# Convolution weights in a ring of six one-bank chunks, first products split by batch, additions spread behind every bank

## The reference

```python
# x: (2, 512, 256), block_values: (128, 64, 64, 16), cols, rows: (128,) in 0..3
xb = x.reshape(batch, n_block_row, 64, t)
x_unfold = xb[:, cols]                      # one block of 64 input channels for each of 128 weights
o = causal_conv1d(x_unfold, block_values)   # 16 taps, 64 in, 64 out, each of the 128 blocks by itself
y = zeros.at[:, rows].add(o)                # summed into the output block that rows names
x = x + y
```

## Time and profile before

| | |
|---|---|
| median of 3 runs | 939.17 us (934.13 to 942.73) |
| profiled execution | 930.08 us, span 928.3 us, mean granted clock 0.996 |
| PE busy | 903.2 us, 97% of the span |
| PEld (weight load) busy | 784.5 us, 85% |
| DVE busy | 540.6 us, 58% |
| ACT busy | 429.8 us, 46% |
| POOL busy | 317.3 us, 34% |
| `wconv` loads | 19 of 1024 KB, 7.3 us to landing; 2 of 512 KB, 4.8 us |
| `wtaps` loads | 16 of 768 KB, 7.9 us to landing |

### The profile page before, as it was taken

The page is one execution under the profiler, slowest core; times in us unless marked ns, Lnnn a source line. Parts: engine busy times, 40 slices in busy tenths (PEclk is TensorE's granted clock), DMA queues, the critical chain, the costliest instruction groups (busy, mean ns, idle before and its releaser), DMA issues. The chain is left out here.

```text
span 928.3 us, 16981 instructions
## 1 busy us (share of the span) xinstructions
PE 903.2 (97%) x5729; PEld 784.5 (85%) x5729; DVE 540.6 (58%) x1360; ACT 429.8 (46%) x945; POOL 317.3 (34%) x286
## 2 busy tenths in 40 slices
PE   9999889999999998999999999999999999999998
PEld 7899757888888886778978997897886888888887
DVE  5899975433333337588678668867875533333333
ACT  3422325433343432576567647646653543433332
POOL 5111012455655563121121202112102256555563
PEclk9999999999999999999999999999999999999999
DMA  8999201111111112000000000000001111111111
GB/s 309 342 354 403 104 11 37 52 51 51 37 48 51 51 34 73 21 23 2 35 23 0 34 0 23 0 0 0 1 1 35 35 52 50 35 51 51 51 34 62
DMA packets 23360, 60.96 MB, mean 66 GB/s; under 512 B 3154, under 2 KB 11028, under 8 KB 20884
## 3 DMA queue, kind: packets, MB, share of 16 engines
q1 hardware_dynamic: 21012, 47.80, 15.4%
q0 software_dynamic: 2304, 12.58, 3.5%
HBM read 59.33 MB, written 1.05 MB: 65 GB/s over the span
## 5 line engine op out<-in xcount | busy, mean ns | idle before, releaser
L822 DVE TENSOR_TENSOR f_h<-f_scaled,bank 128x512 f32<-128x512 f32 (+1 forms) x90 | 60.9, 676 | 183.5 <-POOL f_scaled L723 183.5
L723 POOL TENSOR_TENSOR f_scaled<-f_act,f_gate_rows 128x512 f32<-128x512 f32 (+1 forms) x90 | 113.5, 1262 | 135.5 <-ACT f_act L654 135.1
L912 PE MATMUL bank<-f_xt_hi,f_w_lo 128*128 128x512 f32 (+1 forms) x400 | 157.0, 393 | 0.0
L912 PE MATMUL bank<-f_xt_hi,f_w_hi 128*128 128x512 f32 (+1 forms) x400 | 156.8, 392 | 0.0
L661 ACT ACTIVATE f_h_hi<-f_h 128x512 fp32r<-128x512 f32 (+2 forms) x102 | 63.6, 624 | 183.6 <-DVE f_h L822 183.6
L912 PE MATMUL bank<-f_xt_lo,f_w_hi 128*128 128x512 f32 (+1 forms) x400 | 123.6, 390 | 0.1
L1091 ACT ACTIVATE at_prob<-bank,at_sbias,at_qrs 128x512 f32<-128x512 f32 (+3 forms) x128 | 77.7, 617 | 85.4 <-DVE at_sbias L1261 85.4
L929 PE MATMUL bank<-f_w_lo,f_h_hi 128*128 128x256 f32 (+1 forms) x400 | 113.2, 283 | 0.0
L929 PE MATMUL bank<-f_w_hi,f_h_lo 128*128 128x256 f32 (+1 forms) x400 | 113.1, 283 | 0.0
L929 PE MATMUL bank<-f_w_hi,f_h_hi 128*128 128x256 f32 (+1 forms) x400 | 113.1, 283 | 0.0
L831 DVE TENSOR_TENSOR f_h_lo<-f_h,f_h_hi 128x512 fp32r<-128x512 f32 (+2 forms) x102 | 70.2, 688 | 73.1 <-ACT f_h_hi L661 73.0
(11 more groups left out here) (186 smaller groups left out, 1996.3 us busy)
## 6 DMA issues: line engine op xcount, KB each, us to landing
cv_raw<-in_wconv SPq DMA_DIRECT2D x19, 1024.0 KB, 7.3
cv_shared<-in_wtaps POOLq DMA_DIRECT2D x16, 768.0 KB, 7.9
f_wraw<-in_w SPq DMA_DIRECT2D x44, 256.0 KB, 2.7
f_wraw<-in_w SPq DMA_DIRECT2D x44, 128.0 KB, 2.5
at_wraw<-in_wqkv SPq DMA_DIRECT2D x3, 768.0 KB, 4.3
at_oraw<-in_wo SPq DMA_DIRECT2D x4, 512.0 KB, 3.6
cv_raw<-in_wconv SPq DMA_DIRECT2D x2, 512.0 KB, 4.8
X<-in_x_tiles SPq DMA_DIRECT2D x2, 512.0 KB, 9.0
```

The lines of the kernel that those rows point to most:

```text
L723: g.tensor_tensor(scaled[half][:, cols], act[half][:, cols], gate_rows[:, half * HALF + cols.start:half * HALF + cols.stop], ALU.mult).the ...
L822: v.tensor_tensor(h_f[half][0:rows, cols], src[half][0:rows, cols], pu[half][0:rows, cols], ALU.mult)\
L912: mm = t.matmul(bank[half][0:rows, :], w, x, start=q == 0, stop=q == len(steps) - 1)
```

## The change

The output of the loads, the sums and the products is the same; their sizes and order differ.

- `raw` is a ring of six buffers of one bank each (512 KB) and not three of two banks; SP issues one load per bank, chunk c when chunk c-6 is summed. The host lays `wconv` out in 40 chunks.
- The products of stage 0 are split by batch: those of batch 0 (256 columns) stand between the last four banks of stage 1, those of batch 1 behind them.
- `xn` is two views, one for each batch, each in its own third of `shared`, so that `wtaps` chunk 1 may be loaded after the splits of batch 0 and chunk 2 after those of batch 1.
- The conversion of the block numbers to `line_pair` on DVE moves into stage 0.
- The additions are counted by block: 16 blocks behind stage 1, then 4 behind each low bank of stage 2 and 5 behind each of stages 3 and 4 (`BANK_BLOCKS`). `load_pairs` comes where a block number is a multiple of 8.

```diff
 NPE, ND = 5, 3
-CO, OB, DB = 16, 8, 8
+OB, DB, RING = 8, 8, 6
 
...
         NW = NCB * NCB
-        CHUNK = CO * P
+        CHUNK = OB * P
         DROW = ND * BS
...
         shared = sb("shared", [P, 3 * DB * DROW], F32)
-        xn = shared[:, 0:NT * D].rearrange("p (n t) -> p n t", n=NT)
         raw_d = [shared[:, i * DB * DROW:(i + 1) * DB * DROW].rearrange("p (n f) -> p n f", n=DB) for i in (2, 0, 1)]
+        xn = [shared[:, b * DB * DROW:b * DB * DROW + GC * D].rearrange("p (n t) -> p n t", n=GC) for b in range(B)]
         xc_hi, xc_lo = sb("xc_hi", [P, NCB, B, XPITCH], F32R), sb("xc_lo", [P, NCB, B, XPITCH], F32R)
-        raw = [sb(f"raw{i}", [P, CHUNK], F32) for i in range(3)]
+        raw = [sb(f"raw{i}", [P, CHUNK], F32) for i in range(RING)]
         ws_hi = [sb(f"ws_hi{i}", [P, NW, BS], F32R) for i in range(2)]
...
-        raw_in = [cm(f"cv_raw_in{i}") for i in range(3)]
+        raw_in = [cm(f"cv_raw_in{i}") for i in range(RING)]
-        first_in = [cm(f"cv_first_in{q}") for q in range(CO // OB)]
-        CB = CO // OB
+        FIRST_BLOCKS, BANK_BLOCKS = 2 * DB, (4, 5, 5)
...
             return (lambda x: x[k * BS:(k + 1) * BS, par::2, b, lo:lo + D],
-                    xn[par * BS:(par + 1) * BS, b * GC:(b + 1) * GC, :])
+                    xn[b][par * BS:(par + 1) * BS, :, :])
 
...
         def _(sp):
-            def blocks_first(c):
-                if c >= 3:
-                    sp.wait_ge(s["summed"], (c - 2) * CB)
-                sp.dma_start(raw[c % 3][:], ins["wconv"][c]).then_inc(raw_in[c % 3], 16)
-
-            sp.dma_start(colrow[:, 0:1], ins["cols"].rearrange("(n a) -> n a", a=1)).then_inc(s["cr_in"], 16)
-            sp.dma_start(colrow[:, 1:2], ins["rows"].rearrange("(n a) -> n a", a=1)).then_inc(s["cr_in"], 16)
-            for q in range(CB):
-                part = slice(q * CHUNK // CB, (q + 1) * CHUNK // CB)
-                sp.dma_start(raw[0][:, part], ins["wconv"][0][:, part]).then_inc(first_in[q], 16)
-            blocks_first(1)
-            sp.dma_start(line[:, 0, :], ins["cols"].rearrange("(a n) -> a n", a=1)).then_inc(s["line_in"], 16)
-            sp.dma_start(line[:, 1, :], ins["rows"].rearrange("(a n) -> a n", a=1)).then_inc(s["line_in"], 16)
+            def bank_blocks(c):
+                if c >= RING:
+                    sp.wait_ge(s["summed"], c - RING + 1)
+                sp.dma_start(raw[c % RING][:], ins["wconv"][c]).then_inc(raw_in[c % RING], 16)
+
             def input_half(b):
...
 
+            sp.dma_start(colrow[:, 0:1], ins["cols"].rearrange("(n a) -> n a", a=1)).then_inc(s["cr_in"], 16)
+            sp.dma_start(colrow[:, 1:2], ins["rows"].rearrange("(n a) -> n a", a=1)).then_inc(s["cr_in"], 16)
+            for c in range(3):
+                bank_blocks(c)
+            sp.dma_start(line[:, 0, :], ins["cols"].rearrange("(a n) -> a n", a=1)).then_inc(s["line_in"], 16)
+            sp.dma_start(line[:, 1, :], ins["rows"].rearrange("(a n) -> a n", a=1)).then_inc(s["line_in"], 16)
+            bank_blocks(3)
             input_half(0)
-            blocks_first(2)
+            for c in range(4, 6):
+                bank_blocks(c)
             input_half(1)
-            for c in range(3, NPE * (BS // CO)):
-                blocks_first(c)
+            for c in range(6, NPE * SB):
+                bank_blocks(c)
             prefetch[0](sp)
...
             for d in range(NDC):
-                if d == 1:
-                    g.wait_ge(s["xc_lo_done"], 4 * B)
+                if d in (1, 2):
+                    g.wait_ge(s["xc_lo_done"], 4 * d)
                 if d >= 3:
...
 
-            def add_blocks(d, pairs):
-                v.wait_ge(raw_d_in[d % 3], 16 * (d // 3 + 1))
-                for n in range(DB):
-                    for k in range(2):
-                        v.wait_ge(s["added"], (d * DB + n) * 2 + k + 1)
-                        part = slice(k * DROW // 2, (k + 1) * DROW // 2)
-                        dst = acc[:, bass.ds(pairs[n], 1), part].rearrange("p a f -> p (a f)")
-                        v.tensor_tensor(dst, dst, raw_d[d % 3][:, n, part], ALU.add).then_inc(s["added"], 1)
+            def add_block(i, pairs):
+                d, n = divmod(i, DB)
+                if n == 0:
+                    v.wait_ge(raw_d_in[d % 3], 16 * (d // 3 + 1))
+                for k in range(2):
+                    v.wait_ge(s["added"], i * 2 + k + 1)
+                    part = slice(k * DROW // 2, (k + 1) * DROW // 2)
+                    dst = acc[:, bass.ds(pairs[n], 1), part].rearrange("p a f -> p (a f)")
+                    v.tensor_tensor(dst, dst, raw_d[d % 3][:, n, part], ALU.add).then_inc(s["added"], 1)
 
...
                 for n in range(b * GC, (b + 1) * GC):
-                    v.tensor_scalar(xn[:, n, :], X[:, n, :], moments[:, n, 0:1], rstd[:, n:n + 1],
+                    v.tensor_scalar(xn[b][:, n - b * GC, :], X[:, n, :], moments[:, n, 0:1], rstd[:, n:n + 1],
                                     ALU.subtract, ALU.mult).then_inc(s["xn_ready"], 1)
...
             variances(0)
-            low_banks(0, range(2, 4))
+            v.wait_ge(s["line_in"], 32)
+            v.tensor_copy(line_f[:], line[:]).then_inc(s["cr_conv"], 1)
+            low_banks(0, range(2, 3))
+            v.wait_ge(s["cr_conv"], 3)
+            v.scalar_tensor_tensor(out=line_pair[:], in0=line_f[:, 0, :], scalar=float(NCB), in1=line_f[:, 1, :],
+                                   op0=ALU.mult, op1=ALU.add).then_inc(s["cr_conv"], 1)
+            low_banks(0, range(3, 4))
             normalize(0)
...
             low_banks(1, range(6, 7))
-            v.wait_ge(s["line_in"], 32)
-            v.tensor_copy(line_f[:], line[:]).then_inc(s["cr_conv"], 1)
-            v.wait_ge(s["cr_conv"], 3)
-            v.scalar_tensor_tensor(out=line_pair[:], in0=line_f[:, 0, :], scalar=float(NCB), in1=line_f[:, 1, :],
-                                   op0=ALU.mult, op1=ALU.add).then_inc(s["cr_conv"], 1)
             v.sem_inc(s["added"], 2)
...
             more = load_pairs(1)
-            add_blocks(0, pairs)
-            add_blocks(1, more)
-            d = 2
+            for i in range(DB):
+                add_block(i, pairs)
+            for i in range(DB, FIRST_BLOCKS):
+                add_block(i, more)
+            done = FIRST_BLOCKS
             for st in range(2, NPE):
-                for i in range(4):
-                    low_banks(st, range(2 * i, 2 * i + 1))
-                    pairs = load_pairs(d)
-                    low_banks(st, range(2 * i + 1, 2 * i + 2))
-                    if i == 3 and d + 1 < NDC:
-                        more = load_pairs(d + 1)
-                        add_blocks(d, pairs)
-                        d += 1
-                        pairs = more
-                    add_blocks(d, pairs)
-                    d += 1
+                for q in range(SB):
+                    low_banks(st, range(q, q + 1))
+                    for i in range(done, done + BANK_BLOCKS[st - 2]):
+                        if i % DB == 0:
+                            pairs = load_pairs(i // DB)
+                        add_block(i, pairs)
+                    done += BANK_BLOCKS[st - 2]
             for st in range(NPE, NST):
...
             def sum_bank(st, q):
-                c, part = st * (BS // CO) + q // CB, q % CB
-                if c > 0 and part == 0:
-                    t.wait_ge(raw_in[c % 3], 16 * (c // 3 + (c % 3 > 0)))
-                if st * SB + q >= BANKS:
-                    t.wait_ge(s["ws_lo_done"], st * SB + q - BANKS + 1)
-                if c == 0:
-                    t.wait_ge(first_in[part], 16)
+                c = st * SB + q
+                t.wait_ge(raw_in[c % RING], 16 * (c // RING + 1))
+                if c >= BANKS:
+                    t.wait_ge(s["ws_lo_done"], c - BANKS + 1)
                 for o in range(OB):
-                    w0 = (part * OB + o) * P
                     m = t.matmul(ps[q % BANKS][:].rearrange("p (w o) -> p w o", o=OB)[:, :, o],
-                                 raw[c % 3][:, w0:w0 + P], onehot[:], start=True, stop=True)
+                                 raw[c % RING][:, o * P:(o + 1) * P], onehot[:], start=True, stop=True)
                 m.then_inc(s["summed"], 1)
 
-            def products(slot, c, r, tap):
+            def products(slot, c, r, tap, half=None):
                 w = c * NCB + 2 * r
-                hi, lo = (x[:, c, :, bass.ds(tap, D)] for x in (xc_hi, xc_lo))
+                batch = slice(0, B) if half is None else slice(half, half + 1)
+                bank = ps[4 + r][:, batch.start * D:batch.stop * D]
+                hi, lo = (x[:, c, batch, bass.ds(tap, D)] for x in (xc_hi, xc_lo))
                 w_hi, w_lo = (x[slot][:, w:w + 2, :].rearrange("p c o -> p (c o)") for x in (ws_hi, ws_lo))
                 for lhs, rhs in ((w_hi, hi), (w_lo, hi), (w_hi, lo)):
-                    t.matmul(ps[4 + r][:], lhs, rhs, start=False, stop=False)
```

(23 more changed lines are left out.)

## The result

| | before | after |
|---|---|---|
| median of the runs | 937.0 us (933.74 to 946.46, 20 runs) | 932.07 us (931.08 to 933.35, 20 runs) |
| ratio after to before | | 0.994 (95% interval 0.9924 to 0.9956) |
| profiled execution | 930.08 us, span 928.3 | 931.38 us, span 929.5 |

The changed kernel is 5 us faster, about 0.6%, where I had said 943.5 and 934 to 948. Two things stand out. The profiled execution went the other way, from 928.3 to 929.5. And the scatter fell from 12.7 us to 2.3. So the gain lies in executions of the kernel before that are not like the one whose rows I read.

What follows compares the result with a forecast made beforehand. DVE was taken to set the convolution's end; exposed register loads would release PE 4.3 us later, at 110.6 instead of 106.35. Median 939.2 + 4.3 gave 943.5 us, range 934 to 948.

Steps and rivals of the forecast that it cites:

- The base of the sum: Whole run: median 939.17 us, 9.1 above the profiled execution's 930.08, with the same distance expected after the change.
- The 0.62 us stall goes; bounds 0 to 0.62: PE's wait for a late raw chunk before stage 2: the ring of six half-size chunks removes it, 0.6 us taken.
- The ceiling of 5.5 us for a perfect change: Convolution phase: all a perfect change could take, 2.91 + 1.7 + 0.62 + 0.30 us, 0.6% of the run.
- What PE won at the start becomes waiting: PE's earlier entry to stage 2 only lengthens its later wait for DVE, to some 8 us (102.5 to 110.6).
- the hole: PE idle from 103.44 to 106.35, 2.91 us, waiting for DVE; forecast to end at 110.6, 4.3 us later.
- Early products: First products split by batch among stage 1 banks: cost +0.1 us, 0.30 us split wait gone, stage 2 at 42.2.
- Register loads: DVE's block-number loads inside groups of additions: eight exposed at 0.57 us each, 4.6 us in all.
- the 0.6 us that DVE was to wait at the start of stage 3: DVE reaches stage 3's first bank at 64.3, but it is rounded at 64.9: 0.6 us added.
- The 0.6 for loads at the head of a group: Six block-number loads behind one low bank on DVE, 0 to 0.17 us each, taken as 6 x 0.1.
- the 60.9 us: DVE from stage 2's first bank to the last addition, 48.53 to 109.45: price of 24 low banks and 224 half additions.
- Low clock behind the hole: PE's slow clock after its wait for DVE: between +1.7 and -1.7 us, taken as 0.
- The DMA rival: Stages 2 to 4: smaller raw transfers carry less, +25 us, giving 964 us; chance 0.08.

Runs made afterwards that it cites:

- c_before: The kernel before, measured once more with no edit: 936.65 us, ratio 1.0021; the traced execution took 936.51 us.
- after2: The changed kernel itself, measured and traced a second time beside the others on one chip: 932.29 us, ratio 0.9958 to the kernel before.
- r_starve: Kernel before with the six-buffer ring alone, chunk 14 asked for late on purpose: 931.77 us, ratio 0.9954.
- b_spread: Kernel before with only the additions spread behind every bank: 938.05 us, ratio 1.0036.
- b_ring: Kernel before with only the ring of six one-bank chunks: 929.64 us, ratio 0.9946.
- b_late: Kernel before with its first wtaps chunk held back until the eight input splits are done: 937.46 us, ratio 0.9993.
- rf: Changed kernel with the spreading of additions undone, ring and early first products kept: 927.59 us, ratio 0.9902, and again 927.21 us, ratio 0.9904.

## Why the prediction was wrong

- **The base of the sum: wrong, and it decided the outcome.** I took the 9.1 us between the profiled execution (930.08) and the median (939.17) as an edge that both kernels carry. The changed kernel carries 0.7 (931.38 and 932.07). The edge was low granted clock, 0.996 in the profiled execution and 0.990 to 0.991 in the middle of later runs, and the ring alone takes it away (929.64 us, every run at 0.995 or 0.996). One such execution was traced (c_before): there it is a `raw` chunk late by 2.01 us with the low clock behind it. That this is so in most of them is not shown, and a chunk made late on purpose gave back only about 2 us. The runs of 934 to 943 us already said that executions differ by more than any wait I had found; I called it scatter. With the profiled execution as base the sum says 934.4, and 931.4 was measured.
- **"The 0.62 us stall goes; bounds 0 to 0.62": the mis-sized term.** The upper bound came from one wait of one execution. In the second trace the same wait is 2.01 us and costs 5.5 us at the start of stage 2, and, through DVE, 6.4 us of the span. Even with 1.7 us more for a low clock the range would have reached down to 932.3 only. The first trace already gave reason to doubt the bound: a chunk was needed 7.3 us after it was asked for, and the slowest `cv_raw` load took 9.8:

```profile
DMA to landing us min/median/max: 4.4/7.3/9.8
```

- **The ceiling of 5.5 us for a perfect change: true of one execution, too low for the median.** It was the sum of the waits of the profiled execution. The version with ring and early products and without the spreading lies 2.5 to 2.9 us below that execution by its medians, but 8.4 and 8.8 us below the medians of the kernel before. Faster by 1% was not beyond the phase.
- **"What PE won at the start becomes waiting": right for the 1 us I meant, wrong for the stall.** A stall before the last bank of stage 1 delays DVE's additions too, so DVE's chain and the hole move with it.
- **Early products: right.** Stage 2 at 41.4 (forecast 42.2; PE began 0.2 earlier), the split waits gone, first bank on DVE at 45.9 (46.3). That they alone would gain 0.38% (0.9962) was not seen. In their trace the chunk of bank 14 has until 34.02 and PE does not wait for it, which fits; whether that is the way of the gain was not tested.
- **Register loads: right in kind, a little high.** Eight at 0.57 us were forecast; six cost 0.59 and two 0.08. DVE's queue runs ahead of the engine by more than the one instruction I allowed for, so a load one block behind a low bank is still covered by it. That is my reading of the 0.08; no run tested it. The last addition came at 109.8 and not 112.6, PE was released at 107.9 and not 110.6: 2.7 us too much. The two loads are 1.0 of it, the earlier start of the additions 0.4, and the 0.6 us that DVE was to wait at the start of stage 3 is not there. The 0.6 for loads at the head of a group was in part counted twice, since the 60.9 us from the kernel before had such loads in it.
- **Low clock behind the hole: taken as equal.** In the first trace it was 6.8 us in place of 3.4, about half of it lying in the wait, so near zero in cost. In the second (after2, 932.86 us) the wait is 6.31 us and the clock is at 0.51 for 6.2 us behind it, some 1.4 us more than in the kernel before, inside the 1.7 allowed.
- **The DMA rival: did not happen.** PE never waited for `raw`. The 40 loads of 512 KB took 6.9 us to landing in the median, under the 9.1 that the ring allows, and in stage 3 the DMA engines moved 378 GB/s at a share of 0.99 (397 at 1.00 before). My reading of the earlier trace rows was wrong: a load of 1024 KB had been issued at 2.6 us, so not only 512 KB chunks were in flight. The rule of at least 1 MiB per DMA (the Trainium skill, DMA: Bandwidth & Descriptors, Rules for kernel authors) is one for the highest bandwidth. This case does not test that bandwidth; it shows only that with several loads in flight half the size was enough, and that the ring with it gained 0.5%.

What stays open: why the chunk near 33 us is late in one execution and hardly in another; by what way the ring gains the 3.6 to 4.2 us that a late chunk does not give back; and where the low clock of the longest executions (938 us and more) lies, of which no trace was taken.

## What to carry to other kernels

When a kernel's runs scatter by more than the waits in its profile add up to, the profile may be of a lucky execution: take a second trace, or set the mean granted clock of each run beside its time, before costing anything. Do not carry the distance between the profiled execution and the median over to the changed kernel as a constant: it was 9.1 us before and 0.7 after. A stall of TensorE is to be priced with the low clock that may follow it: here a wait of 2.0 us in place of 0.6 went with 6.4 us more of span, one of 1.6 in place of none with 3.3. A ring of more and smaller buffers on the same memory took the scatter away here. Registers that an engine loads for its addresses belong directly behind a long instruction in the engine's program, where its run time covers them, and not between dependent short ones (0.08 us or less against 0.59).

## What the runs showed of the hardware

The length of a wait did not fix the low clock behind it. On PE, waits of 1.57 and 2.01 us were followed by 9.8 us at half clock (r_starve, c_before) and one of 1.06 by 6.8 us (b_spread). Waits of 0.62 and 0.30 us were followed by none. The same wait of 1.35 us was followed by none in b_ring and by 3.4 us in b_late. Holes of 2.2 to 2.9 us were followed by 3.4 us in the kernel before, c_before and rf, and by none in b_ring (2.48), r_starve (2.23) and b_late (2.92). The Trainium skill (TensorE: Matmul & The Clock Gate, Part 1) says that the low clock is the default which activity lifts, and that the same kernel meets a different number of slow matmuls from run to run. The scatter of the kernel before agrees: its twelve runs in c_before have mean granted clocks from 0.982 to 0.995.
